# Self-attention inside a decoder layer: each projection waits for its own weights, and four copies and splits change their place in the step

## What is computed

```python
h = 16                                        # heads of 64
q = split_heads(x @ Wq + bq, h)               # x here is layernorm(x)
k = split_heads(x @ Wk + bk, h)
v = split_heads(x @ Wv + bv, h)
pattern = einsum('bhid,bhjd->bhij', k, q) * scale
prob = softmax(pattern, axis=-2)
out = einsum('bhis,bhid->bhsd', prob, v)
return concat_heads(out) @ Wo + bo            # then x = x + this
```

## Time and the profile before

| what | value |
|---|---|
| median of 3 runs | 3564.81 us (3563.89 to 3568.51) |
| the profiled execution, its own time | 3561.65 us |
| its span, first to last instruction | 3559.7 us |
| mean granted TensorE clock | 0.967 |
| PE busy | 3233.0 us (91%) |
| DVE busy | 2578.7 us (72%) |
| ACT busy | 2279.3 us (64%) |
| POOL busy | 1076.8 us (30%) |

### The profile page before, as it was taken

The page is one execution under the profiler, slowest core; times in us unless marked ns, Lnnn a source line. Parts: engine busy times, 40 slices in busy tenths (PEclk is TensorE's granted clock), DMA queues, the critical chain, the costliest instruction groups (busy, mean ns, idle before and its releaser), DMA issues.

```text
span 3559.7 us, 47086 instructions
## 1 busy us (share of the span) xinstructions
PE 3233.0 (91%) x15056; PEld 2498.3 (70%) x15056; DVE 2578.7 (72%) x4060; ACT 2279.3 (64%) x4138; POOL 1076.8 (30%) x1177
## 2 busy tenths in 40 slices
PE   5899999999999999977999999988989999941998
PEld 4777777777787878765666666655768888831887
DVE  5887777777777777756787878877963369876564
ACT  4786766666676767644777777766442256678765
POOL 1223232323333333333655655656500000000000
PEclk9999999999999999988999999999999999975999
DMA  3344433433443443327575656664712268889764
GB/s 119 137 152 139 127 125 116 149 115 125 131 134 113 134 135 117 113 71 137 110 127 114 121 115 126 120 99 152 252 74 107 107 216 296 288 332 397 274 244 183
DMA packets 269955, 555.47 MB, mean 156 GB/s; under 512 B 28025, under 2 KB 105857, under 8 KB 255377
## 3 DMA queue, kind: packets, MB, share of 16 engines
q1 hardware_dynamic: 265488, 544.08, 51.8%
q10 hardware_dynamic: 4224, 8.39, 0.6%
HBM read 322.72 MB, written 162.30 MB: 136 GB/s over the span
## 4 chain that ended last, share of the span: by engine, by line
PE 39%; DVE 6%; issue 5%; DMA 2%; ACT 1%; POOL 1%; SPq 0%; DVEq 0%; ACTq 0%; POOLq 0%
PE gu_acc L2436 15%; PE ca_mx L2351 3%; PE md_acc L2516 2%; PE md_acc L2517 2%; PE md_acc L2518 2%; DVE ca_negm L1953 2%; PE ca_pj L2331 2%; PE ca_ov L2381 2%; PE ca_ov L2382 2%; PE ca_st L2369 2%; PE ca_pj L2318 2%; DVE ca_el L1968 1%; PE ca_ms L2341 1%; DMA ca_q<-ca_ql 1%; DVE ca_eh L1962 1%
## 5 line engine op out<-in xcount | busy, mean ns | idle before, releaser
L816 POOL TENSOR_SCALAR sa_ex<-sa_ex,sa_rs 128x512 f32<-128x512 f32 x512 | 356.9, 697 | 939.6 <-DVE sa_rs L658 939.6
L653 DVE TENSOR_REDUCE sa_nm<-sa_st 128x1 f32<-128x512 f32 x512 | 351.6, 687 | 274.2 <-PE sa_st L941 273.0
L514 ACT ACTIVATE sa_eh<-sa_tr 128x512 fp32r<-128x512 f32 x512 | 306.8, 599 | 294.5 <-PE sa_tr L951 291.2
L898 PE MATMUL sa_pj<-sa_xh,sa_w 128*128 128x512 f32 x1536 | 456.9, 417 | 22.9 <-DVE sa_kl L636 11.1
L507 ACT ACTIVATE sa_ex<-sa_st,sa_nm 128x512 f32<-128x512 f32 x512 | 351.1, 686 | 59.7 <-DVE sa_nm L653 56.9
L1953 DVE TENSOR_REDUCE ca_negm<-ca_mx 128x2 fp32r<-128x1024 f32 x256 | 312.7, 1222 | 100.8 <-PE ca_mx L2351 97.1
L662 DVE TENSOR_TENSOR sa_el<-sa_tr,sa_eh 128x512 fp32r<-128x512 f32 x512 | 351.5, 686 | 39.0 <-ACT sa_eh L514 32.1
L2225 POOL TENSOR_TENSOR ca_el<-ca_ex,ca_eh 128x512 fp32r<-128x512 f32 x256 | 352.4, 1378 | 59.7 <-ACT ca_eh L1737 59.4
L1729 ACT ACTIVATE ca_ex<-ca_st 128x512 f32<-128x512 f32 x512 | 296.4, 586 | 40.0 <-PE ca_st L2369 38.5
L898 PEld LDWEIGHTS sa_pj<-sa_xh,sa_w 128*128 128x128 f32 x1536 | 262.3, 190 | 68.4 <-issue 26.5
L951 PE MATMUL sa_tr<-top_ident,sa_ex 128*128 128x128 f32 x2048 | 306.3, 272 | 0.7 <-POOL sa_ex L816 0.7
(11 more groups left out here) (292 smaller groups left out, 7510.8 us busy)
## 6 DMA issues: line engine op xcount, KB each, us to landing
sa_w<-w_split SPq DMA_DIRECT2D x56, 1536.0 KB, 7.5
gate<-gu_ev SPq DMA_DIRECT2D x24, 1024.0 KB, 4.4
gu_g<-gate SPq DMA_DIRECT2D x48, 512.0 KB, 5.8
gate<-gu_g SPq DMA_DIRECT2D x48, 512.0 KB, 3.5
up<-gu_ev SPq DMA_DIRECT2D x24, 1024.0 KB, 5.7
md_a<-gate SPq DMA_DIRECT2D x96, 256.0 KB, 6.8
md_b<-up SPq DMA_DIRECT2D x96, 256.0 KB, 7.4
md_a<-gate SPq DMA_DIRECT2D x44, 512.0 KB, 15.3
```

Source lines behind the costliest of these rows:

```text
L514: nc.scalar.activation(eh[:, v % 2], tr[:, v % 2], ACT.Copy).then_inc(act_eh, 1)
L653: nc.vector.tensor_reduce(nm[:, u % U:u % U + 1], st[:, u % 2], AX_X, ALU.max, negate=True).then_inc(dve_mx, 1)
L816: nc.gpsimd.tensor_scalar(ex[:, u % U], ex[:, u % U], rs[:, u % U:u % U + 1], 1.0, ALU.mult, ALU.mult).then_inc(pool_n, 1)
L898: yield nc.tensor.matmul(pj[:, bank], w[:, n % 2, m, part, k], xx[:, b % 2, k], start=(i == 0 and k == 0), stop=(i == 2 and k == DK - 1))
```

## The change

Four engines' orders change, and no arithmetic does.

1. PE: the key projection of pairs 0 to 7 waits for the key weights' split alone (count 3n+1 in place of 3n+3); the query and value projections get waits of their own (3n+2, 3n+3).
2. DVE: `low_out` moves from before `low_key` to behind `low_exponent` (`el`) in step 5. DVE's `split_weights` moves behind `aggregate`, `out_normalised` and `normalised` of its step.
3. ACT: `transposed_out` moves from the head of step 5 to behind the exponential of step 5; `high_heads` moves from step 4 (behind `high_key`) to step 5, behind `transposed_out` and ahead of `high_query`.
4. POOL: `low_heads` moves from step 5 to step 6.

```diff
 # ACT
-                if t == 5 and out_tile(s, 1) is not None:
-                    transposed_out(out_tile(s, 1))
                 if t == 7 and norm_tile(s, 0) is not None:
                     transposed_x(norm_tile(s, 0))
                 if 0 <= G - TR < U * N:
                     high_exponent(G - TR)
                 if 0 <= G < U * N:
                     exponent(G)
+                if t == 5 and out_tile(s, 1) is not None:
+                    transposed_out(out_tile(s, 1))
+                if t == 5 and out_tile(s, -1) is not None:
+                    high_heads(out_tile(s, -1))
                 if t in (3, 5, 7) and 0 <= s and s + 2 < HP:
                     split_weights(s + 2, t // 2 - 1)
                 if t == keys_at(s) and s + 1 < N:
                     high_key(s + 1, 0)
                     high_key(s + 1, 1)
-                if t == 4 and out_tile(s, -1) is not None:
-                    high_heads(out_tile(s, -1))
 # DVE
-                if t == 5 and out_tile(s, 1) is not None:
-                    low_out(out_tile(s, 1))
                 if t == 7 and norm_tile(s, 0) is not None:
                     low_x(norm_tile(s, 0))
...
                 if 0 <= G - TR < U * N:
                     low_exponent(G - TR)
+                if t == 5 and out_tile(s, 1) is not None:
+                    low_out(out_tile(s, 1))
                 if t == 0 and norm_tile(s, 0) is not None:
                     statistics(norm_tile(s, 0))
-                if t in (3, 5, 7) and 0 <= s and s + 2 < HP:
-                    split_weights(s + 2, t // 2 - 1)
                 if t == 1 and norm_tile(s, 0) is not None:
                     aggregate(norm_tile(s, 0))
                 if t == 3 and out_tile(s, 1) is not None:
                     out_normalised(out_tile(s, 1))
                 if t == 3 and norm_tile(s, 0) is not None:
                     normalised(norm_tile(s, 0))
+                if t in (3, 5, 7) and 0 <= s and s + 2 < HP:
+                    split_weights(s + 2, t // 2 - 1)
 # POOL
-                if t == 5 and out_tile(s, -1) is not None:
+                if t == 6 and out_tile(s, -1) is not None:
                     low_heads(out_tile(s, -1))
 # PE, start_projection(n, m)
                 if m == KM:
                     if n < HP:
-                        e.wait_ge(act_w, 3 * n + 3)
-                        e.wait_ge(dve_w, 3 * n + 3)
+                        e.wait_ge(act_w, 3 * n + KM + 1)
+                        e.wait_ge(dve_w, 3 * n + KM + 1)
...
                 elif m == QM:
+                    if n < HP:
+                        e.wait_ge(act_w, 3 * n + QM + 1)
+                        e.wait_ge(dve_w, 3 * n + QM + 1)
...
                 else:
+                    if n < HP:
+                        e.wait_ge(act_w, 3 * n + VM + 1)
+                        e.wait_ge(dve_w, 3 * n + VM + 1)
                     e.wait_ge(act_k, 2 * n + 2)
                     e.wait_ge(dve_k, 2 * n + 2)
```

## The result

The kernel after takes **3549.61 us** (median of 5 runs, 3545.49 to 3552.61) against 3564.81 before: ratio 0.9952, 95% interval 0.9941 to 0.9963, so 15.2 us faster; forecast were 18.4. Its profiled execution took 3545.49 us (span 3543.5, mean granted clock 0.967).

The account below looks back on a forecast made before the run. PE was taken to bound self-attention, so only its stalls count. 9.6 + 1.9 + 13.0 - 5.2 - 0.9 = 18.4 us off the profiled 3561.65 gives 3543.2; plus 3.2 for the median, 3546.4 us, range 3538 to 3559.

Parts of the forecast that it names:

- Part 1: Step 0 of pairs 1 to 6: the key projection's wait for the value weights' split goes, gaining 9.6 us net.
- Part 2: Step 3, pairs 2 to 5: DVE normalises while waiting for ACT's split, then splits; gains 1.9 us.
- Part 3: s mod 8 = 3 and 4, 14 pairs: `low_key` ahead of `low_out` on DVE removes a PE stall, gaining 13.0 us.
- Part 4: ACT's later `high_heads` loses 5.2 us in s mod 8 = 1; `xo` behind the exponential loses 0.9 in s mod 8 = 6.
- Part 5: POOL's `low_heads` at step 6 in place of 5 costs nothing.
- the first batch gives its gain back: Rival, pairs 0 to 7: step 0's stall only moves to `heads` at steps 2 and 6; 3555.9 us, chance 0.12.
- the later batches gain nothing: Rival, s mod 8 = 3 and 4: ACT's `osb` over 0.9 us late, `low_key` gain zero; 3559.4 us, chance 0.08.
- the slower rival: `low_heads` on POOL beside DVE's `heads` holds DVE up 2.40 us for each of 28 tiles; 3613 us, chance 0.03.

Follow-up runs that it names:

- E1: The kernel before with only PE's finer waits of the three projections for their weights' splits: 3557.33 us, ratio 0.9976.
- E2: The kernel before with only DVE's `low_out` moved behind `low_exponent`, ACT and POOL as before: 3553.90 us, ratio 0.9970.
- E4: The kernel after with `high_heads` back at step 4 and `low_heads` back at step 5, `transposed_out` left as in after: 3543.22 us, ratio 0.9942.
- E7: The kernel after with `low_heads` alone back at step 5: 3546.78 us, ratio 0.9947.
- E3: The kernel after with ACT's and POOL's orders of before: 3544.32 us, ratio 0.9939.
- E8: E3 with `low_out` at step 6 behind `heads` for s mod 8 below 6, unchanged for s mod 8 = 6: 3532.13 us, ratio 0.9906.
- E6: E5 with the first batch's split of the query weights at step 6 in place of 5 on ACT and DVE: 3536.40 us, ratio 0.9920.
- E5: E3 with `low_out` at step 6 behind `heads`: 3535.88 us, ratio 0.9919.

## Why the prediction was right

Right in its direction, its mechanism and nearly every term, with one row misread (the 12.1 us above). Term by term:

| step | forecast | measured | from |
|---|---|---|---|
| Part 1 | -9.6 | -9.5 | before to E1 |
| Part 2 | -1.9 | -1.8 | E1 to after |
| Part 3 | -13.0 | -12.8 (14 pairs, 0.92 each) | after; -13.0 in E2 |
| Part 4, s mod 8 = 1 | +5.2 | +4.7 (6 x 0.73 + 0.34) | after, E4 with E7 |
| Part 4, s mod 8 = 6 | +0.9 | +0.8 | after, E3 |
| Part 5 | 0 | 0 | E7 |
| elsewhere | 0 | +0.2 | after |
| sum | -18.4 | -18.4 | |

"Elsewhere" is s mod 8 = 7, 0.03 for each pair, mostly. The traces show -19.2 by the last `scores`: the sum, and 0.8 from the start of pair 0. The key projection of pair 0 starts at the same time in both (38.07 in before, 38.09 in after), released by DVE's low part of an input tile and not by the weights whose wait was changed. Its matmuls first start 0.43 apart and then 0.23, and the turn came earlier in after. In the ten traces the first `scores` lies between 48.29 (after) and 49.69 (E1), and these two have the same waits of PE; so the 0.8 is scatter and no effect of the change.

**Part 1.** Pair 4 of after, step 0: the key projection starts at 130.40, right behind the transposes, and no longer waits for the split that starts at 131.58. Of the weights' wait nothing is left, and what the prediction named as late next is there.

```profile
130.40 1.41 PE L898 MATMUL sa_pj<-sa_xh,sa_w 128*128 128x512 f32 x5
...
131.58 0.68 DVE L604 TENSOR_TENSOR sa_w<-sa_w_raw,sa_w 128x512 fp32r<-128x512 f32 x1
...
132.43 0.69 POOL L816 TENSOR_SCALAR sa_ex<-sa_ex,sa_rs 128x512 f32<-128x512 f32 x1 [3.11 <-DVE sa_rs L658]
133.18 0.42 PEld L957 LDWEIGHTS sa_tr<-top_ident,sa_ex 128*128 128x128 f32 x4 [0.42 <-POOL sa_ex L816]
...
136.82 0.73 DVE L675 SCALAR_TENSOR_TENSOR sa_on<-sa_ov,sa_bv,sa_osb 64x512 f32<-64x512 f32 x1
...
137.70 0.47 PE L968 MATMUL sa_ov<-sa_eh,sa_va 128*128 128x512 f32 x1 [0.17 <-DVE sa_on L675]
```

The turn of step 1 waits for `divide`, and the `product` of step 2 for `heads`, both a little. How much came back can be counted. In pair 4 of before the key projection starts 2.32 us behind the start of the transposes ahead of it, and 0.35 in after; by this distance the stall was 1.8, 1.65 and four times 1.96 us in pairs 1 to 6, 11.3 in all. E1's six pairs gain 9.4. So 1.9 came back: 0.1 to 0.2 in each of pairs 1, 2 and 6, and 0.47 in each of 3 to 5, of which about 0.2 at the turn and 0.25 at the `product`. The forecast had taken 1.8 off its 11.4. Its working isn't clean there: it writes that 0.45 comes back in pairs 2 to 5, but its two times (144.05 and 143.7) and its sum (1.9 less 0.35 is 1.55) take 0.35. The measured 0.47 is near the written one. Pair 2 gained 0.2 more than forecast (1.5 for 1.3) and the other five together 0.35 less, so the sum is a little better than its parts.

The rival that *the first batch gives its gain back* needed 9.5 us more to come back than the forecast had. It had the place right (`heads` at step 2) and the size wrong. The likely reason is that DVE, busy 80% of the batch, has a gap before most maxima (1.00 and 0.29 us at steps 1 and 2 of pair 4 in before), and there a delay ends; no experiment tests it by itself.

**Part 2.** In pair 3, step 3, `normalised` (118.83) now runs in the time that DVE spent waiting for ACT's split (118.75 to 119.38), and DVE's split follows without a gap; in the earlier trace rows it was the other way round.

```profile
118.75 0.63 ACT L467 ACTIVATE sa_w<-sa_w_raw 128x512 fp32r<-128x512 f32 x1
...
118.83 0.54 DVE L625 TENSOR_SCALAR sa_xn<-sa_xr,sa_mv,sa_rstd 128x512 f32<-128x512 f32 x1
...
119.41 0.69 DVE L604 TENSOR_TENSOR sa_w<-sa_w_raw,sa_w 128x512 fp32r<-128x512 f32 x1
```

**Part 3.** Pair 28, steps 5 and 6 of after, to be read beside the earlier trace rows. The pair's step 5 begins 14.64 us earlier here than there.

```profile
706.03 1.52 DVE L636 SCALAR_TENSOR_TENSOR sa_kl<-sa_pj,sa_bias,sa_ks 64x512 fp32r<-64x512 f32 x2
...
707.16 0.59 ACT L532 ACTIVATE sa_xo<-sa_ms 128x512 fp32r<-128x512 f32 x1
...
707.63 1.06 ACT L526 ACTIVATE sa_oh<-sa_o 128x1024 fp32r<-128x1024 f32 x1
...
708.19 0.68 DVE L704 TENSOR_TENSOR sa_xol<-sa_ms,sa_xo 128x512 fp32r<-128x512 f32 x1
...
708.34 1.65 PE L898 MATMUL sa_pj<-sa_xh,sa_w 128*128 128x512 f32 x6
...
708.72 0.60 ACT L520 ACTIVATE sa_osb<-sa_ov 64x512 f32<-64x512 f32 x1
...
709.56 0.74 DVE L675 SCALAR_TENSOR_TENSOR sa_on<-sa_ov,sa_bv,sa_osb 64x512 f32<-64x512 f32 x1
...
710.45 0.47 PE L968 MATMUL sa_ov<-sa_eh,sa_va 128*128 128x512 f32 x1 [0.46 <-DVE sa_on L675]
```

The prediction's chain, moved by 14.64, has `heads` at 709.55, `osb` at 708.57 and `product` at 710.43; the trace has 709.56, 708.72 and 710.45. The value projection (708.34) idles no more. `osb` is 0.15 later than forecast, inside the 0.38 of air. So *the later batches gain nothing* failed by its own condition: `osb` would have had to be 0.9 late.

**Part 4.** Pair 25 of after against the earlier trace rows: with `high_heads` in front, the query copy and `osb` slide, and DVE stands idle 0.75 for `osb`, PE 0.53 for DVE. In all, DVE's idle time in front of `heads` for `osb` is 3.6 us in before and 9.0 in after.

```profile
628.78 1.05 ACT L526 ACTIVATE sa_oh<-sa_o 128x1024 fp32r<-128x1024 f32 x1
629.73 0.67 ACT L487 ACTIVATE sa_qs<-sa_pj,sa_bias 64x512 fp32r<-64x512 f32 x1
629.91 2.38 POOL L821 TENSOR_TENSOR sa_ol<-sa_o,sa_oh 128x1024 fp32r<-128x1024 f32 x1
630.43 0.59 ACT L520 ACTIVATE sa_osb<-sa_ov 64x512 f32<-64x512 f32 x1
631.05 0.74 DVE L675 SCALAR_TENSOR_TENSOR sa_on<-sa_ov,sa_bv,sa_osb 64x512 f32<-64x512 f32 x1 [0.75 <-ACT sa_osb L520]
```

The term was 0.07 too large for each pair (0.73 for 0.8). I added the whole 1.06 of `high_heads` to the chain, but ACT's instructions follow each other by less than their durations: 0.95 between the starts of `high_heads` and the query copy. In s mod 8 = 6 DVE waits 0.46 for `xo`, as forecast, and most of it is air before the next maximum (E4 parts it from `high_heads`).

**Part 5 and the slower rival.** The same `heads`, over all 116 of its kind, in before and in after (ns, shortest, median, longest):

```profile
L675 DVE SCALAR_TENSOR_TENSOR sa_on<-sa_ov,sa_bv,sa_osb x116: 732/743/745, 74.9 to 1573.5; 64x512 f32<-64x512 f32 x116
```
```profile
L675 DVE SCALAR_TENSOR_TENSOR sa_on<-sa_ov,sa_bv,sa_osb x116: 732/743/746, 72.3 to 1554.3; 64x512 f32<-64x512 f32 x116
```

In after `low_heads` (629.91 to 632.29 above) starts ahead of `heads` (631.05) and runs across it, and the 0.74 stays 0.74. The rival needed 0.91 us more for each tile, and there is nothing of it. E7 moves `low_heads` away and changes nothing. The Trainium skill (SBUF — State Buffer, "Who interferes with whom") says that a DVE instruction with at most one input in SBUF, outside the 2-port perf modes, doesn't contend with GpSimd. `heads` has one of its two tiles in PSUM, and these rows agree.

**The 3.2 us between forecast and median.** The sum of the terms was met, so they aren't the cause. The profiled execution came out 2.3 above its forecast (3545.5 for 3543.2): 3.0 more behind, 0.8 less at the start. The other 0.9 is the step from a profiled execution to a median, 3.2 in before and 4.1 in after. The part behind isn't changed in any of the ten kernels and measures 2000.9 to 2006.9. In before and after PE's waits there for one transfer, of cross-attention's queries, differ by 3.0:

```profile
PE ca_mx L2351 <- DMA ca_q<-ca_ql: 6.2, 1, 6.2
```
```profile
PE ca_mx L2357 <- DMA ca_q<-ca_ql: 9.2, 2, 7.4
```

But E3 has 9.4 in the same place and is the shortest behind, so this wait doesn't explain the length of the part. Whether the 3 us are scatter or come from the earlier start is **open**: no experiment held self-attention's end fixed while it changed something else.

## What to carry to other kernels

When a stall is to be removed, write out what stands ahead of the releaser on its engine and what PE meets next: done for each place in the loop, this gave every term within 0.5 us here. One order for all places is rarely the best: `low_out` behind `heads` gains 0.43 where the step is full of matmuls and costs 0.79 where it is not, and splitting the case brought 3532.1 (E8). Undo the parts of a bundle one by one even when it wins: ACT's two moves cost 5.5 us here, and the gain didn't need them.

## What was not expected of the hardware

**A stretch at the lower clock, in some executions only.** Pair 63 takes 23.0 to 23.2 us in the profiled executions of E1, E2, E6, E7 and E8, and 21.6 in those of before, after, E3, E4 and E5. PE idles 2.63 us in front of the `product` of step 2 of this pair in all ten. In before it goes on at once at full speed; the window has a granted clock of 1.00:

```profile
1543.50:1549.30 5.80, 5.80 (x30) 4.79 (x31) 2.55 (x6) 2.70 (x8) 3.41 (x5) 1.00 0.02 3
```

In E1 the same window has 0.71, and 21 matmul records in place of 30:

```profile
1534.70:1540.50 5.80, 5.80 (x21) 4.68 (x22) 2.04 (x5) 2.47 (x7) 2.21 (x4) 0.71 0.01 3
```

Its timeline shows the turn: behind the idle 2.63 the matmuls start 0.23 apart, then 0.42 to 0.43, then 0.23 again from 1539.76 on.

```profile
1534.65 0.47 PE L968 MATMUL sa_ov<-sa_eh,sa_va 128*128 128x512 f32 x1 [2.63 <-DVE sa_on L675]
...
1536.50 0.63 PE L996 MATMUL sa_pj<-sa_wo_hi,sa_xh 128*128 128x512 f32 x1
1536.92 0.63 PE L946 MATMUL sa_st<-sa_ks,sa_qs 128*128 128x512 f32 x1
1537.35 0.63 PE L947 MATMUL sa_st<-sa_kl,sa_qs 128*128 128x512 f32 x1
```

That is the level of 1.2 GHz in place of 2.4, and its price is 1.6 us. In E2, E6 and E8 the window shows 0.71 too; in E7 it shows 0.75, with the slow starts right behind the idle time, and the price is 1.4. The Trainium skill (TensorE: Matmul & The Clock Gate, "Wait — 56ns, not 53.3ns?") gives 427 ns between starts for 512 columns at the lower level, and these rows agree. This stretch is nearly all of the 1.7 by which E1's later batches are longer than before's, and of the 1.6 between E2 and E3. What decides between the two in kernels with the same idle time is open; E7 is after with one operation moved, and has the slow stretch where after has none.

**Some instructions start before the one ahead of them has ended.** In pair 25 the query copy starts 0.95 us behind `high_heads`, which takes 1.05; in pair 28 `low_out` starts 0.61 behind an `el` that takes 0.69. But in pair 30 of E5 `low_out` follows a `heads` of 0.74 only after 0.77. So a chain is best made of distances between starts from the same pair of operations, and not of durations. The Trainium skill (ScalarE: Activation LUTs, "What ACT_TABLE_LOAD costs") says that ACTIVATEs in a row overlap by some 93 ns; the 0.10 here agrees.
